# Gated cross-attention block: mask matmuls on 32-row tiles, two mask transfers a group, another order on the SP queue

## What is computed

```python
x = x + tanh(g_xattn) * attention(layernorm(x), ctx, ctx, mask)      # 16 heads of 8
x = x + tanh(g_ffn)   * experts(layernorm(x))
# attention
scores = einsum('bhqd,bhkd->bhqk', q, k) / sqrt(HD)
scores = where(mask[:, None, :, :], finfo.min, scores)
attn = softmax(scores); merged = (attn @ v) merged over heads; out = merged @ Wo.T + bo
# experts: 8, FF = 512, gelu; gate weights thresholded and normalised
h  = gelu(einsum('td,edf->etf', x, W1) + b1); eo = einsum('etf,efd->etd', h, W2) + b2
out = einsum('te,etd->td', w, eo)
```

## Time and profile before

| | |
|---|---|
| median of 3 runs | 627.77 us (626.75 to 628.27) |
| profiled execution | 625.05 us, of which the span from first to last instruction is 623.2 us |
| attention, until about | 247 us of the span |
| PE busy | 593.8 us (95%) |
| DVE, ACT, POOL busy | 479.4, 378.6, 178.9 us |
| mean granted clock of TensorE | 0.981 |

### The profile page before, as it was taken

One profiled execution on the slowest core, in us unless ns is written; L12 is line 12 of the kernel. 1 busy time (PEld: TensorE's weight loads), 2 busy tenths in 40 slices (PEclk: granted clock), 3 DMA queues, 4 the chain that ended last, 5 costly groups with the idle time before them and its releaser, 6 DMA issues.

```text
span 623.2 us, 13765 instructions
## 1 busy us (share of the span) xinstructions
PE 593.8 (95%) x4490; PEld 452.0 (73%) x4490; DVE 479.4 (77%) x940; ACT 378.6 (61%) x625; POOL 178.9 (29%) x224
## 2 busy tenths in 40 slices
PE   7699899999999998999999999999999999999998
PEld 6556566666666655788878788787887887887886
DVE  3457677777776776578879788888888888888886
ACT  2134455555555545767777677677677676776673
POOL 7523344444444221212113212212112112121121
PEclk9969899999999999999999999999999999999999
DMA  6854556555655520041121121111121121111210
GB/s 183 223 150 129 153 160 175 142 141 151 172 150 152 160 64 5 3 102 44 44 68 35 56 68 52 50 57 44 50 67 50 34 67 50 50 61 40 67 51 17
DMA packets 43998, 55.12 MB, mean 88 GB/s; under 512 B 9520, under 2 KB 27824, under 8 KB 42416
## 3 DMA queue, kind: packets, MB, share of 16 engines
q1 hardware_dynamic: 43504, 53.99, 30.5%
q10 hardware_dynamic: 448, 0.53, 0.2%
HBM read 39.16 MB, written 14.81 MB: 87 GB/s over the span
## 4 chain that ended last, share of the span: by engine, by line
PE 82%; DMA 6%; ACT 4%; SPq 4%; DVE 2%; issue 2%; ACTq 0%; DVEq 0%
PE ps_h L1059 10%; PE ps_h L1061 9%; PE ps_h L1060 9%; PE ps_y L1074 9%; PE ps_y L1076 9%; PE ps_y L1075 9%; PE misc L1037 4%; DMA kq_st<-maxT 4%; PE scores L975 4%; PE scores L1003 3%; PE scores L1015 3%; PE scores L992 2%; ACT probs L559 2%; PE misc L1114 1%; DMA kq_scratch<-kq_parts 1%
## 5 line engine op out<-in xcount | busy, mean ns | idle before, releaser
L583 ACT ACTIVATE h_sb<-ps_h,b_sb 128x512 f32<-128x512 f32 x256 | 176.1, 690 | 102.1 <-PE ps_h L1061 92.1
L742 DVE TENSOR_TENSOR h_low<-h_sb,h_high 128x512 fp32r<-128x512 f32 x256 | 164.5, 682 | 0.1
L522 POOL TENSOR_TENSOR yT<-yT,weighted 128x512 f32<-128x512 f32 x54 | 70.9, 1313 | 277.9 <-DVE weighted L917 277.9
L738 DVE CAST h_high<-h_sb 128x512 fp32r<-128x512 f32 x128 | 97.7, 763 | 52.9 <-ACT h_sb L583 52.7
L719 DVE TENSOR_REDUCE neg_max<-scores 128x8 f32<-128x1024 f32 x64 | 77.9, 1221 | 49.1 <-PE scores L975 49.1
L1059 PE MATMUL ps_h<-x_high,w_high 128*128 (+1 forms) x256 | 101.9, 398 | 2.1 <-ACT h_sb L583 2.0
L1074 PE MATMUL ps_y<-h_high,w_high 128*128 128x512 f32 x256 | 100.2, 391 | 0.3 <-ACT h_high L587 0.3
L1061 PE MATMUL ps_h<-x_high,w_low 128*128 (+1 forms) x256 | 99.8, 390 | 0.0
L1076 PE MATMUL ps_y<-h_high,w_low 128*128 128x512 f32 x256 | 99.7, 389 | 0.0
L1060 PE MATMUL ps_h<-x_low,w_high 128*128 (+1 forms) x256 | 99.7, 389 | 0.0
L1075 PE MATMUL ps_y<-h_low,w_high 128*128 128x512 f32 x256 | 99.6, 389 | 0.0
(11 more groups left out here) (127 smaller groups left out, 720.9 us busy)
## 6 DMA issues: line engine op xcount, KB each, us to landing
w_row<-w_scratch SPq DMA_DIRECT2D x64, 256.0 KB, 3.1
kq_st<-kq_scratch SPq DMA_DIRECT2D x64, 192.0 KB
kq_scratch<-kq_parts SPq DMA_DIRECT2D x30, 256.0 KB, 3.2
w_raw<-in_w_ffn SPq DMA_DIRECT2D x16, 256.0 KB, 3.7
kq_scratch<-kq_parts SPq DMA_DIRECT2D x32, 128.0 KB, 3.3
ctx_sb<-in_ctx SPq DMA_DIRECT2D x16, 128.0 KB, 2.6
out_y<-y_out SPq DMA_DIRECT2D x7, 256.0 KB, 2.3
x_all<-in_x SPq DMA_DIRECT2D x13, 128.0 KB, 2.2
```

What stands on the lines that cost most here:

```text
L583: nc.scalar.activation(h_sb[:, j % HBUF, :], ps_h[:, j % 4, :], ACT.Gelu_apprx_tanh, bias=b1_sb[:, j:j + 1]).then_inc(h_done, 1)
L738: nc.vector.tensor_copy(h_high[:, j % HBUF, :], h_sb[:, j % HBUF, :]).then_inc(high_odd, 1)
L742: nc.vector.tensor_tensor(h_low[:, j % HBUF, :], h_sb[:, j % HBUF, :], h_high[:, j % HBUF, :].bitcast(F32), ALU.subtract).then_inc(low2_do ...
```

## The change

- The mask of a bank is no longer one matmul over 128 rows. Row tile r of the array adds it in four pieces j = 0 to 3. In `natural_mask` a piece is a 32x32 tile that writes partitions 32j to 32j+31 over all 512 columns; the two banks of a pair alternate, so eight matmuls on eight different tiles follow each other. In `transposed_mask` a piece has 32 rows and writes 128 partitions and 128 columns (four runs of 32).
- For that each row tile needs the whole mask of a batch: `mask_words` holds it once for each of four partition groups, loaded by two DMAs a group (64 KB each, rows of 512 B) in place of one (32 KB, rows of 128 B). It is one buffer now; the load of group g waits for the cast of group g-1. The cast on POOL has 1024 elements a partition in place of 256.
- Query 4i+j now stands at place 32j+i. The turning of `xn` writes its columns so (`dealt`), and ScalarE puts them back in the copies to `headsT`.
- SP's order: max1; masks and context; `stacks`; max0; then the expert weight and x; `stores`. Six loads of later weights go from the end of `stacks` of group 1 to the end of iteration 0.
- Zero matmuls: 6 instead of 2 ahead of the first max0, and 3 new ones ahead of the first `transposed`.
- `merged`, `mergedT` and `x2n` have one buffer instead of two, each with a wait for the group before.

```diff
-        mask_words = sa("mask_words", [P, 2, GB, S // 4], I32)
-        mask_b = sa("mask_b", [P, 2, GB, S], BF16)
+        mask_words = sa("mask_words", [P, GB, S], I32)
+        mask_b = sa("mask_b", [P, 2, GB, 4, S], BF16)
...
+            def load_mask(g):
+
+                for b in range(GB):
+                    every = bass.AP(a["mask"].tensor, (g * GB + b) * 32 * S, [[0, ROWS], [S, 32], [1, S]])
+                    sp.dma_start(mask_words[:, b, :], every).then_inc(mask_in[g % 2], 16)
...
+            def masks_and_contexts(it):
+
+                if (g := group_at(it, 1)) is not None:
+                    if g > 0:
+                        sp.wait_ge(mask_done, g)
+                        load_mask(g)
...
-                    pool.wait_ge(mask_in[u], g // 2 * 16 + 16)
+                    pool.wait_ge(mask_in[u], g // 2 * 32 + 32)
                     wait_count(pool, tr_rest_full, 2 * (g - 2) + 2)
-                    nc.gpsimd.tensor_copy(mask_b[:, u, :, :], mask_words[:, u, :, :].bitcast(U8)).then_inc(mask_done, 1)
+                    nc.gpsimd.tensor_copy(mask_b[:, u, :, :, :].rearrange("p b j k -> p b (j k)"), mask_words[:].bitcast(U8)).then_inc(mask_done, 1)
...
-            def natural_mask(r, b, u):
-                return mm(scores[:, r, :].rearrange("p (s k) -> p s k", s=SLABS), masked_ident[:],
-                          mask_b[:, u, b, :].unsqueeze(1).to_broadcast([P, SLABS, S]), start=False, stop=True)
+            def natural_mask(pair, b, u):
+
+                for j in range(4):
+                    for r in pair:
+                        rows = slice(32 * r, 32 * r + 32)
+                        ins = mm(scores[32 * j:32 * j + 32, r, :].rearrange("p (s k) -> p s k", s=SLABS), masked_ident[rows, rows],
+                                 mask_b[rows, u, b, j, :].unsqueeze(1).to_broadcast([32, SLABS, S]), start=False, stop=True)
+                return ins
...
-                natural_mask(0, b, u)
-                natural_mask(1, b, u).then_inc(nat_rest_full, 1)
-
-            def transposed_mask(r, b, u):
-                return mm(scores[:, 2 + r, :].rearrange("p (s q) -> p s q", s=SLABS), mask_b[:, u, b, :],
-                          masked_ident[:].unsqueeze(1).to_broadcast([P, SLABS, S]), start=False, stop=True)
+                natural_mask((0, 1), b, u).then_inc(nat_rest_full, 1)
+
+            def transposed_mask(pair, b, u):
+
+                for j in range(4):
+                    for r in pair:
+                        rows = slice(32 * r, 32 * r + 32)
+                        ins = mm(scores[:, 2 + r, :].rearrange("p (s j i) -> p j s i", s=SLABS, j=4)[:, j], mask_b[rows, u, b, j, :],
+                                 masked_ident[rows, rows].unsqueeze(1).to_broadcast([32, SLABS, 32]), start=False, stop=(j == 3))
+                return ins
```

More of the change, by code:

```diff
@@ L148, in gated_block @@
         sums_r = sa("sums_r", [P, GB * H], F32)
-        merged = sa("merged", [P, 2, GB * H, HD], F32)
-        mergedT = sa("mergedT", [P, 2, GT], F32)
+        merged = sa("merged", [P, GB * H, HD], F32)
+        mergedT = sa("mergedT", [P, GT], F32)
         x_biased = sa("x_biased", [P, GB, D], F32)
@@ L154, in gated_block @@
         rstd2 = sa("rstd2", [P, 2, GB], F32)
-        x2n = sa("x2n", [P, 2, GB, D], F32)
+        x2n = sa("x2n", [P, GB, D], F32)
         x2T = sa("x2T_sb", [P, 2, GT], F32)
@@ L365, in inputs_ahead @@
                         sp.dma_start(ctx_sb[:, u, :, :], ctx_v[g]).then_inc(ctx_in[u], 16)
[L366 to L373, removed]
             def stacks(it):
@@ L386, in stacks, with weights_and_x @@
                                      kq_dram[g, 24 * r:24 * r + 24, :]).then_inc(kq_in[g % 3], 16)
-                    if g == 1:
-                        later_weights()
+            def weights_and_x(it):
+                if (g := group_at(it, 2)) is not None:
+                    u = g % 2
+                    if g > 0:
+                        wait_count(sp, wsplit_done, g - 1)
+                        sp.dma_start(w_raw[:, u, :], a["w_ffn"][g]).then_inc(w_in[u], 16)
+                if (g := group_at(it, 6)) is not None:
+                    if g >= 4:
+                        if g >= 8:
+                            sp.wait_ge(ln1_aggr, (g - 3) * GB)
+                        sp.dma_start(x_all[:, g * GB:(g + 1) * GB, :], x_v[g]).then_inc(x_group_in[g % 4], 16)
             def stores(it):
@@ L599, in body @@
                     misc_wait_full(act, "merged", g)
-                    if g >= 2:
-                        misc_wait_full(act, "wo", g - 2)
-                    nc.scalar.activation(mergedT[:, u, :], misc[:, bank_of("merged"), 0:GT], ACT.Copy).then_inc(misc_read[bank_of("merged")], 1)
+                    if g >= 1:
+                        misc_wait_full(act, "wo", g - 1)
+                    nc.scalar.activation(mergedT[:], misc[:, bank_of("merged"), 0:GT], ACT.Copy).then_inc(misc_read[bank_of("merged")], 1)
                 if (g := group_at(it, -3)) is not None:
@@ L793, in body @@
                     dve.wait_ge(recip_done, g + 1)
-                    if g >= 2:
-                        misc_wait_full(dve, "merged", g - 2)
-                    nc.vector.tensor_tensor(merged[:, u, :, :], hv[:, :, 0:HD], sums_r[:].unsqueeze(2).to_broadcast([P, GB * H, HD]),
+                    if g >= 1:
+                        misc_wait_full(dve, "merged", g - 1)
+                    nc.vector.tensor_tensor(merged[:], hv[:, :, 0:HD], sums_r[:].unsqueeze(2).to_broadcast([P, GB * H, HD]),
                                             ALU.mult).then_inc(misc_read[bank_of("heads")], 1)
@@ L865, in body @@
                     dve.wait_ge(rstd2_done, g + 1)
-                    if g >= 2:
-                        misc_wait_full(dve, "x2T", g - 2)
+                    if g >= 1:
+                        misc_wait_full(dve, "x2T", g - 1)
                     for b in range(GB):
-                        nc.vector.tensor_scalar(x2n[:, u, b, :], x_all[:, g * GB + b, :],
+                        nc.vector.tensor_scalar(x2n[:, b, :], x_all[:, g * GB + b, :],
                                                 mean_var2[:, u, b, 0:1], rstd2[:, u, b:b + 1], ALU.subtract, ALU.mult).then_inc(x2n_done, 1)
@@ L960, in _, with dealt @@
             mm = nc.tensor.matmul
+            def dealt(t):
+                return t.rearrange("p (j i) -> p i j", j=4)
             def turn(what, g, src, n=GB):
@@ L965, in turn @@
                 for b in range(n):
-                    ins = nc.tensor.transpose(misc[:, k, b * S:(b + 1) * S], src(b), ident[:])
+                    out = misc[:, k, b * S:(b + 1) * S]
+                    ins = nc.tensor.transpose(dealt(out) if b >= GB else out, src(b), ident[:])
                 ins.then_inc(misc_full[k], 1)
@@ L1092, in body @@
                     misc_wait_read(pe, "heads", g)
-                    turn("merged", g, lambda b: merged[:, u, b * H:(b + 1) * H, :].rearrange("p h d -> p (h d)"))
+                    turn("merged", g, lambda b: merged[:, b * H:(b + 1) * H, :].rearrange("p h d -> p (h d)"))
                 if (g := group_at(it, -3)) is not None:
@@ L1098, in body @@
                         pe.wait_ge(g_copied, 1)
-                    turn("x2T", g, lambda b: x2n[:, u, b, :])
+                    turn("x2T", g, lambda b: x2n[:, b, :])
                     if g == NG - 1:
@@ L1113, in body @@
                     for b in range(GB):
-                        ins = mm(misc[:, bank_of("wo"), b * D:(b + 1) * D], mergedT[:, u, b * S:(b + 1) * S], wo_sb[:], start=True, stop=True)
+                        ins = mm(misc[:, bank_of("wo"), b * D:(b + 1) * D], mergedT[:, b * S:(b + 1) * S], wo_sb[:], start=True, stop=True)
                     ins.then_inc(misc_full[bank_of("wo")], 1)
```

39 lines of the change are left out of this document (19 added, 20 removed).

## The result

The changed kernel takes 662.12 us (659.34 to 666.18, 4 runs) against 627.26 us for the one before: a ratio of 1.059, 95% interval 1.049 to 1.068. The profiled execution took 663.53 us, the span 661.6 us. The forecast was 614 us.

What follows compares the result with a forecast made beforehand. One ring through all engines, 13.88 us a group, was taken as the bound. From the profiled 625.05 us, 5.9 (ring) and 8.0 (beginning) leave 611.2; the median's 2.7 makes 613.9, say 614 us, range 607 to 624.

Steps and rivals of the forecast that it cites:

- Natural and transposed masks by tiles: Mask matmuls in attention: overlapping tile pieces gain 0.15 us at each of two natural places and 0.15 at the transposed one.
- The ring: Dependency loop through all engines, one attention group long (13.88 us): 0.45 us shorter a group, 5.9 us in all.
- full clock from 16 to 75 us: Sign that the forecast is right: TensorE at 2.4 GHz throughout this stretch, which before had two stretches at half clock.
- the mask loads: Two mask transfers a group on SP instead of one: about 0.45 us more issue and 96 KB more a group.
- B: Theory tested in the follow-ups: gaps in which PE waits (order on SP, copies, buffers, transfers) let the clock fall.
- The beginning: First iterations: zero matmuls keep the clock up and maxima land sooner, gaining 8.0 us, between 0 and 10.
- Copies to headsT: ScalarE's strided copies, in the shadow: taken at 0, between -0.05 and +0.2 us each.
- Single buffers and dealt turns: Buffers wait only for PE's work one iteration ago; two strided turns up to 0.3 us longer, taken at 0.
- lower bound of 607 us: Low end of the 8-in-10 range: the beginning gains 10 us and natural places 0.21 us each.
- Mine for slower: Rival: column pieces of one row tile run one after another, 0.88 us a natural place, 633 us; chance 0.08.
- A clock that falls elsewhere: Rival: the ring shortens but new gaps in the first iterations drop the clock, beginning unchanged, 622 us; chance 0.14.

Runs made afterwards that it cites:

- e13: e10 with the mask loads moved to the end of SP's iteration, behind the stores: 615.22 us, ratio 0.986.
- e12: e7 with the mask loads moved behind the stores, one group earlier: 621.02 us, ratio 0.995.
- e11: The changed kernel with the mask loads moved to the end of SP's iteration, behind the stores: 642.74 us, ratio 1.031.
- e17: e11 with five unused whole-array matmuls of 512 columns added an iteration: 618.12 us, ratio 0.988.
- e7: The changed kernel with all mask matmuls back on the whole array and 96 KB of mask loads a group: 633.81 us, ratio 1.020.
- e10: The changed kernel with only three of eight mask places by tiles, the others whole, and plain copies to headsT: 636.72 us, ratio 1.020.
- e4: The changed kernel with plain copies to headsT, the value matmuls' output pattern strided instead: 666.21 us, ratio 1.069.
- e1: The kernel before with only the changed order on SP and the added zero matmuls: 619.13 us, ratio 0.989.
- e18: e12 with every mask matmul over 256 of its 512 columns, half of the scores unmasked: 621.43 us, ratio 0.989.

## Why the prediction was wrong

- **Natural and transposed masks by tiles: right.** Mask to values 0.34 us (0.35 to 0.42 named), eight in 0.41 us (about 0.45), scores to max0 0.21 us shorter (0.15). The period with a gate is 13.10 us in e13 (13.3 to 13.5 forecast). The ring gave back 0.6 us a group in the changed kernel and 0.8 in e13, not 0.45. The Trainium skill, TensorE: Matmul & The Clock Gate, section "Wait — 56ns, not 53.3ns?", has starts never below about 25 ns apart. The estimate from it is that eight pieces spread over 0.175 us. The trace disagrees where tiles differ: all eight stand in 0.41 us, the first alone in 0.39.
- **The step that failed: the removed matmuls were priced as time alone.** I read the clock's two falls as caused by gaps of PE, filled one of them, and carried "full clock from 16 to 75 us" and beyond as given. But sixteen whole-array matmuls of 512 columns were taken from each period of 13.88 us. With them e12 has a clock of 1.00 from 75 to 240 us; with tiles in their place e11 has 0.85; with five unused ones added e17 has no fall between 44 and 218 us. In ratio, e11 less e12 is 0.036, some 22 us, with what the shorter ring gives already taken off (e11 loads 128 KB of masks a group, e12 96 KB, both behind the stores).
- **The second: the mask loads, costed at nothing beyond 0.45 us of issue.** I named what stands behind the new wait on SP (context, `stacks`, max0) and didn't price the delay. The wait for max0 was the largest that PE had for a transfer, and larger loads now stood ahead of it. Loads ahead instead of behind: 0.025 in ratio with whole masks (e7 less e12, 15 us), 0.028 with tiles (changed kernel less e11, 17 us), 0.035 with three places by tiles (e10 less e13, 21 us). A part of that is clock too, so B was not all wrong: from 75 to 240 us e7 has 0.96 and e12 1.00, the changed kernel 0.76 and e11 0.85. By which path the loads lower it in the changed kernel, which hardly waits for maxima there, stays open.
- **The beginning: right in its first part.** The clock holds from 28 to 38 us and group 1 starts at 36.77 in place of 37.54 (35.4 forecast). By the medians the order gives 4.9 us, with the zeros 6.6, of 8.0. In the changed kernel the wait for max0 came back, 3.35 us at 50.82, and the clock is 0.79 from 44 to 75 us.
- **Copies to headsT: 0.24 us each, above my bound of 0.2, and worth nothing** (e4, e10). Single buffers and dealt turns: e12 against e1 is 0.995 to 0.989, some 3 us, which has the copies and a second cast in it too and is hardly clear of the noise.
- **The range.** The lower bound of 607 us doesn't follow from its terms: 627.8 less 10 for the beginning, less 13 groups at 0.42 for the natural places and 0.22 for the transposed one, is 609.5. It changes nothing in the verdict.
- **The rivals.** Mine for slower was that tiles don't overlap; they do. A clock that falls elsewhere stood in the list of rivals too, but with gaps as its only cause, the beginning as its only place, and 622 us as its time. The falls came in the steady groups, which no rival named.

That the clock falls when the whole-array mask matmuls are taken out of this kernel, and comes back when unused ones are put in, is shown. How much of them it needs is not. The runs of one kernel differ in how often the clock falls, so a stretch of one profile is a rough measure, and the medians decide.

## What to carry to other kernels

A matmul that is removed or made smaller on a TensorE that is mostly at full clock may be what keeps it there: before removing it, ask what else occupies the whole array in that period, and shorten it only where it lies on the ring, leaving it whole in the shadow (with late loads, three of eight places by tiles gave 0.986 here, all eight 1.031). Unused whole-array matmuls in places where PE waits are a quick test of whether a slow-down is the clock's. A load that isn't urgent belongs behind the transfer that others wait for, even if it is small: 96 KB a group ahead of 768 KB and max0 cost 15 us here (e7 and e12).

## What the runs showed of the hardware

- Eight matmuls on 32x32 tiles, 512 bf16 columns each, in two row groups stand in 0.41 us, the first of them alone in 0.39 us (changed kernel at 78.46 us).
- PE's busy time didn't tell the clock here: 151.45 us busy of 165 at 0.85 (e11), 154.94 at 1.00 (e12), 146.60 at 0.94 (e18).
- Writing a PSUM bank with a stride of 32 columns cost PE nothing that the timeline shows: two turns of `xn` take 0.38 us in the changed kernel, as in the one before. ScalarE's copy with a stride of four elements in its SBUF output takes 620 ns (changed kernel) instead of 383 (e4).
- A cast of 1024 elements a partition on POOL takes 1.04 us (changed kernel) where 256 took 0.40.
